# Second feed-forward stage: down product from fp16 parts, issued two tiles behind, low halves on VectorE

## What is computed

```python
def ffn(x):                                    # x: (4, 1024, 128) after a layer norm
    weights = routing_weights(x, Wr, temperature)      # (b, t, 8), from sigmoid and top 2
    gate = einsum('btd,edi->beti', x, Wg)              # 8 experts, 128 inner features each
    up   = einsum('btd,edi->beti', x, Wu)
    h = silu(gate) * up
    e_out = einsum('beti,eid->betd', h, Wd)            # the down product
    return einsum('bte,betd->btd', weights, e_out)

x = x + 0.5 * ffn(layernorm(x))
x = x + attention(layernorm(x))                # 16 heads of 64, latent q and kv, rope
x = x + 0.5 * ffn(layernorm(x))                # the second feed-forward stage
```

## Time and profile before

| | |
|---|---|
| median of 3 runs | 1598.68 us (1597.41 to 1603.1) |
| the profiled execution | 1597.2 us |
| its span | 1595.4 us, mean granted clock of TensorE 0.988 |
| TensorE matmul busy | 1536.4 us, 96% |
| VectorE busy | 1392.0 us, 87% |
| GpSimd busy | 1300.1 us, 81% |
| ScalarE busy | 1219.4 us, 76% |
| second feed-forward stage, turns 0 to 3 | about 1443 to 1595 us of the span |

### The profile page before, as it was taken

One profiled execution on the slowest core, in us unless ns is written; L12 is line 12 of the kernel. 1 busy time (PEld: TensorE's weight loads), 2 busy tenths in 40 slices (PEclk: granted clock), 3 DMA queues, 4 the chain that ended last, 5 costly groups with the idle time before them and its releaser, 6 DMA issues.

```text
span 1595.4 us, 47669 instructions
## 1 busy us (share of the span) xinstructions
PE 1536.4 (96%) x18968; PEld 1018.3 (64%) x18968; DVE 1392.0 (87%) x2860; ACT 1219.4 (76%) x1698; POOL 1300.1 (81%) x910
## 2 busy tenths in 40 slices
PE   5999779999999999999999999999999999989999
PEld 3777435666666666666666666666666666656776
DVE  7567788999999999999999999999999998966453
ACT  4443477888888888888888888888888888883432
POOL 2555356999999999999999999999999997764555
PEclk9999989999999999999999999999999999999999
DMA  7333030212121111212121212111121212003343
GB/s 209 114 115 119 27 80 11 52 32 55 46 54 42 41 42 42 55 39 51 32 51 32 60 42 53 42 41 42 45 55 35 51 32 52 22 2 107 121 136 117
DMA packets 65723, 95.63 MB, mean 60 GB/s; under 512 B 11744, under 2 KB 24544, under 8 KB 65248
## 3 DMA queue, kind: packets, MB, share of 16 engines
q1 hardware_dynamic: 62416, 91.66, 21.4%
q10 hardware_dynamic: 3088, 0.92, 0.3%
HBM read 39.72 MB, written 2.36 MB: 26 GB/s over the span
## 4 chain that ended last, share of the span: by engine, by line
PE 79%; DVE 3%; ACT 2%; POOL 2%; issue 2%; DMA 0%; POOLq 0%; SPq 0%; DVEq 0%
PE ps L965 14%; PE ps L939 14%; PE ps L966 14%; PE ps L985 8%; PE ps L987 8%; PE ps L983 8%; PE ps L954 3%; PE ps L490 2%; PE ps L947 2%; PE ps L933 2%; PE ps L932 2%; POOL area L617 1%; DVE area L1098 1%; PE ps L474 1%; PE ps L476 1%
## 5 line engine op out<-in xcount | busy, mean ns | idle before, releaser
L1303 POOL TENSOR_TENSOR area<-area 128x1024 f16<-128x1024 f32 (+1 forms) x512 | 833.0, 1645 | 89.2 <-ACT area L1223 79.5
L1098 DVE TENSOR_REDUCE area<-ps 128x1 f32<-128x512 f32 x1024 | 665.1, 685 | 10.0 <-PE ps L939 7.6
L1221 ACT ACTIVATE area<-ps 128x1024 f16<-128x1024 f32 x512 | 525.1, 1026 | 141.8 <-PE ps L966 141.5
L985 PE MATMUL ps<-cv_all,area 128*128 128x64 f16 x4096 | 457.6, 195 | 0.0
L983 PE MATMUL ps<-cv_all,area 128*128 128x65 f16 x4096 | 455.7, 193 | 0.6 <-POOL area L1303 0.5
L987 PE MATMUL ps<-cv_all,area 128*128 128x65 f16 x4096 | 454.6, 193 | 0.0
L985 PEld LDWEIGHTS ps<-cv_all,area 128*128 128x128 f16 x4096 | 381.9, 97 | 79.0 <-issue 0.3
L983 PEld LDWEIGHTS ps<-cv_all,area 128*128 128x128 f16 x4096 | 384.6, 97 | 59.5 <-issue 9.0
L939 PE MATMUL ps<-area 128*128 128x512 f16 x1024 | 389.0, 381 | 5.6 <-DVE area L1098 5.3
L965 PE MATMUL ps<-area 128*128 128x512 f16 x1024 | 389.4, 380 | 2.3 <-ACT area L1223 0.6
L966 PE MATMUL ps<-area 128*128 128x512 f16 x1024 | 389.7, 381 | 0.0
(11 more groups left out here) (182 smaller groups left out, 2169.5 us busy)
## 6 DMA issues: line engine op xcount, KB each, us to landing
area<-area SPq DMA_DIRECT2D x384, 128.0 KB, 2.7
area<-f_w_rows_in_dram SPq DMA_DIRECT2D x126, 256.0 KB, 3.2
xg<-in_x SPq DMA_DIRECT2D x4, 512.0 KB, 9.6
out_x<-xg SPq DMA_DIRECT2D x3, 512.0 KB, 4.7
area<-in_wup SPq DMA_DIRECT2D x1, 1024.0 KB, 8.8
cs<-in_rope SPq DMA_DIRECT2D x1, 1024.0 KB, 9.5
area<-area SPq DMA_DIRECT2D x64, 2.0 KB
area<-in_wg SPq DMA_DIRECT2D x1, 512.0 KB, 6.8
```

The costliest lines, as they stand in the source:

```text
L985: nc.tensor.matmul(o[:, 0:DH], p_hi[:, s % 4, c:c + P], latents[:, DH + 1:CV], start=False, stop=False, skip_group_check=True)
L1098: nc.vector.tensor_reduce(mx[:, hd, kh, qt:qt + 1], bank, AX.X, ALU.max).then_inc(s_mr, 1)
L1221: nc.scalar.activation(p_hi[:, s % 4, :], sc, ACT.Exp, scale=0.125).then_inc(s_e16, 1)
L1303: nc.gpsimd.tensor_tensor(p_lo[:, s % 4, c0:], src[:, (s // 2) % 2, :], p_hi[:, s % 4, c0:], ALU.subtract).then_inc(s_pp, 1)
```

## The change

- The first stage is left as it is, but for four operations: in its turns 1 and 2, `down_high` (ScalarE, step 13) and `down_low` (GpSimd, step 15) make fp16 high and low parts of the down weights, each for 4 experts.
- In the second stage hw is also split: ScalarE copies it to fp16 (`hw_hi`), VectorE subtracts (`hw_lo`), three buffers each. The down product is high times high, high times low, low times high, 12 fp16 products of 128 columns in place of 4 of fp32.
- Down runs two tiles behind (`lag = 2`): TensorE's step k is gate_up of tile i+2, then down of tile i-2. VectorE makes the low half of tile i-1 right behind hw of tile i. The last turn ends with two more downs.
- In the second stage the preparation of the next turn is moved: the transposes go to bank 5, at step 1 and at step 15 of the turn before (in the first turn steps 0 and 1); `normed` runs a turn ahead, at steps 8 and 9, in the first two turns, and at steps 0 and 1 of the first turn ahead of silu; hi at steps 0 and 2, router at 3, logits and tanh at 4, route with 6 links a step from step 5 (was 8 from step 7), weight_rows and rows at 10, add_y at 2 and 10.

```diff
+        wd_hi, wd_lo = sb("wd_hi", [P, E, P], F16), sb("wd_lo", [P, E, P], F16)
...
-        big = 30 * 1024
+        big = 30 * 1024 - 800
...
+        def down_high(act, n):
+            act.wait_ge(s_w[3], 16)
+            nc.scalar.copy(wd_hi[:, 4 * n:4 * n + 4, :], wd32[:, 4 * n:4 * n + 4, :]).then_inc(s_wdh, 1)
+
+        def down_low(pool, n):
+            pool.wait_ge(s_wdh, n + 1)
+            part = slice(4 * n, 4 * n + 4)
+            nc.gpsimd.tensor_tensor(wd_lo[:, part, :], wd32[:, part, :], wd_hi[:, part, :], ALU.subtract).then_inc(s_wdl, 1)
...
+            if name == "f2":
+                hw_hi, hw_lo = (carve(3 * 512, F16).rearrange("p (s n) -> p s n", s=3) for _ in range(2))
...
+            lag = 0 if first else 2
...
-                return 6 if first and p == 0 and a == 1 else 7
+                return 6 if first and p == 0 and a == 1 else 5 if not first and p > 0 else 7
...
+                    elif first and p > 0:
+                        pe.wait_ge(s_y, 2 * p - 1)
                     elif p > 0:
-                        pe.wait_ge(s_y, 2 * p - 1)
+                        pe.wait_ge(s_wt, p)
...
+                    if not first and p > 0:
+                        pe.wait_ge(s_y, 2 * p - 1)
...
-                    pe.wait_ge(s_hw, i + 1)
+                    if first:
+                        pe.wait_ge(s_hw, i + 1)
+                    else:
+                        pe.wait_ge(s_wdl, 2)
+                        pe.wait_ge(s_hl, i + 1)
                     for j in range(4):
...
+                            nc.tensor.matmul(o, hw_hi[:, i % 3, tokens], wd_hi[:, e, :], start=(e == 0 and j == 0), stop=False,
+                                             skip_group_check=True)
+                            nc.tensor.matmul(o, hw_hi[:, i % 3, tokens], wd_lo[:, e, :], start=False, stop=False, skip_group_check=True)
+                            last = nc.tensor.matmul(o, hw_lo[:, i % 3, tokens], wd_hi[:, e, :], start=False, stop=(e == E - 1),
+                                                    skip_group_check=True)
...
-                        if not last and k == 5:
+                        if not last and k == (5 if first else 3):
                             router(t + 1)
-                        down(i, t, k, last)
-                        if not last and k in (1, 3):
-                            transpose(t + 1, (k - 1) // 2)
-                        if not last and k == 11:
+                        if first:
+                            down(i, t, k, last)
+                        elif k >= lag:
+                            down(i - lag, t, k - lag, last)
+                        elif t > 0:
+                            down(i - lag, t - 1, 16 + k - lag, False)
+                        if first and not last and k in (1, 3):
+                            transpose(t + 1, k // 2)
+                        if not first and not last and (k == 1 or k == 0 and t == 0):
+                            transpose(t + 1, k)
+                        if not first and t < B - 2 and k == 15:
+                            transpose(t + 2, 0)
+                        if not last and k == (11 if first else 10):
                             weight_rows(t + 1)
+                    if last and not first:
+                        down(t * 16 + 14, t, 14, True)
+                        down(t * 16 + 15, t, 15, True)
...
+                        if not first and t == 0 and k < 2:
+                            normed(1, k)
                         if not (last and k == 15):
                             silu(i + 1, *((t, k + 1) if k < 15 else (t + 1, 0)))
+                        if not first:
+                            act.wait_ge(s_hw, i + 1)
+                            if i > 0:
+                                act.wait_ge(s_dn, i)
+                            nc.scalar.copy(hw_hi[:, i % 3, :], hw[:, k % 2, :]).then_inc(s_hh, 1)
...
+                        if first and t in (1, 2) and k == 13:
+                            down_high(act, t - 1)
                         if not last:
-                            if k in (0, 1):
+                            if first and k in (0, 1):
                                 normed(t + 1, k)
-                            if k in (2, 4):
-                                hi(t + 1, (k - 2) // 2)
-                            if k == 6:
+                            if not first and t < B - 2 and k in (8, 8 + 1):
+                                normed(t + 2, k - 8)
+                            if k in ((2, 4) if first else (0, 2)):
+                                hi(t + 1, (k - 1) // 2 if first else k // 2)
+                            if k == (6 if first else 4):
...
-                            if k == 11:
+                            if k == (11 if first else 10):
                                 rows(t + 1)
...
+                        if first and t in (1, 2) and k == 15:
+                            down_low(pool, t - 1)
...
+                def low_half(i):
+                    v.wait_ge(s_hh, i + 1)
+                    if i > 0:
+                        v.wait_ge(s_dn, i)
+                    nc.vector.tensor_tensor(hw_lo[:, i % 3, :], hw[:, i % 2, :], hw_hi[:, i % 3, :], ALU.subtract).then_inc(s_hl, 1)
...
-                    after_[1].append((lambda: add_y(t, 1)) if t > 0 else (lambda: v.sem_inc(s_y, 1)))
-                    after_[9].append(lambda: add_y(t, 0))
+                    after_[1 if first else 2].append((lambda: add_y(t, 1)) if t > 0 else (lambda: v.sem_inc(s_y, 1)))
+                    after_[9 if first else 10].append(lambda: add_y(t, 0))
...
+                        between[3 if first else 1].append(lambda: lo(t + 1, 0))
+                        between[5 if first else 3].append(lambda: lo(t + 1, 1))
+                        after_[6 if first else 4].append(lambda: logits(t + 1))
+                        jobs = [(route(t + 1), {k: 8 for k in range(7, 11)} if first else {k: 6 for k in range(5, 12)})]
...
-                        v.wait_ge(s_dn, i + 1)
+                        if first:
+                            v.wait_ge(s_dn, i + 1)
+                        elif i >= 2:
+                            v.wait_ge(s_hl, i - 1)
                         nc.vector.tensor_tensor(hw[:, b, :], gw[:, b, :], ps[:, 2 + b, :], ALU.mult).then_inc(s_hw, 1)
+                        if not first and i > 0:
+                            low_half(i - 1)
...
                     turns(turn)
+                    if not first:
+                        low_half(16 * B - 1)
                     add_y(B, 1)
```

More of the change, by code:

```diff
@@ L412, in turn @@
                         weights_to_all(t * 16 + k, t, k)
-                        if not last and k == 15:
+                        if not last and k == (15 if first else 15):
                             rows_out(t + 1)
@@ L451, in weight_rows @@
                     pe.wait_ge(s_routed, p + 1)
-                    if p > 0:
+                    if first and p > 0:
                         pe.wait_ge(s_y, 2 * p)
-                    nc.tensor.transpose(ps[0:E * TB, 6, 0:P], w_by_expert.rearrange("p e t -> p (e t)"), ident[:]).then_inc(s_wr, 1)
+                    nc.tensor.transpose(ps[0:E * TB, 6 if first or p == 0 else 5, 0:P], w_by_expert.rearrange("p e t -> p (e t)"), ident[:]).then_inc(s_wr, 1)
                 def row_on_all(k):
@@ L487, in down @@
                             pe.wait_ge(s_zr, t + 2)
-                    pe.wait_ge(s_hw, i + 1)
-                    for j in range(4):
-                        last = nc.tensor.matmul(ps[:, 6 + k // E, P * j:P * j + P], hw[:, b, P * j:P * j + P], wd32[:, e, :],
-                                                start=(e == 0 and j == 0), stop=(e == E - 1), skip_group_check=True)
+                    if first:
[3 more added lines that the diff above has]
+                        pe.wait_ge(s_hl, i + 1)
+                    for j in range(4):
+                        o, tokens = ps[:, 6 + k // E, P * j:P * j + P], slice(P * j, P * j + P)
+                        if first:
+                            last = nc.tensor.matmul(o, hw[:, b, tokens], wd32[:, e, :], start=(e == 0 and j == 0), stop=(e == E - 1),
+                                                    skip_group_check=True)
+                        else:
+                            nc.tensor.matmul(o, hw_hi[:, i % 3, tokens], wd_hi[:, e, :], start=(e == 0 and j == 0), stop=False,
+                                             skip_group_check=True)
+                            nc.tensor.matmul(o, hw_hi[:, i % 3, tokens], wd_lo[:, e, :], start=False, stop=False, skip_group_check=True)
+                            last = nc.tensor.matmul(o, hw_lo[:, i % 3, tokens], wd_hi[:, e, :], start=False, stop=(e == E - 1),
+                                                    skip_group_check=True)
                     last.then_inc(s_dn, 1)
@@ L562, in rows @@
                     act.wait_ge(s_wr, p + 1)
```

(14 more changed lines are left out.)

3 lines of the change are left out of this document (added).

## The result

The changed kernel takes 1600.96 us (median of 20 runs, 1599.77 to 1605.65), the kernel before 1598.9 us (20 runs beside it): ratio 1.0016, 95% interval 1.0009 to 1.0024. It is slower by 2.6 us, a sixth of a percent, and lies inside the bound of 0.5% that I called no change. The forecast was 1600.9 us. That the two agree to a tenth of a microsecond is luck: executions of the changed kernel differ by up to 6 us.

A forecast was written before the change was run, and what follows sets the result against it. TensorE alone was taken to bound the second feed-forward stage. The terms -14.0 (down), +13.4 (stalls), +2.5 (start) and +0.3 (tail) sum to +2.2 us, giving 1600.9 us, range 1587 to 1613.

The forecast's parts named there:

- The down product: Second stage, TensorE: 12 fp16 products take 0.67 us instead of 0.89 for fp32, 64 times, -14.0 us.
- Quiet tiles: Second-stage tiles without preparation: GpSimd product plus low half need 1.96 us, just within TensorE's 1.97, so they cost nothing.
- The sum of the stalls: First three turns of the second stage: TensorE stalls of 5.8, 3.8 and 3.8 us, together +13.4 us.
- hi and lo: First three turns: second hi cast behind step 2's copy, lo in front of hw(3), which delays hw(3) by 0.45 us.
- tanh: First three turns: logits behind a low half, then tanh and abs in front of silu(6), 1.0 us.
- Routing: VectorE, steps 7 to 9 of the first three turns: links with hw and low half cost 1.7 us a turn.
- Normed: ScalarE, first two turns: normed ahead of silu(10) and silu(11); the first hides behind routing, the second shows with 0.6 us.
- Start: Second stage's start: silu(2) queued behind copy, hi and normed(1, 1), so hw(2) ends late, +2.5 us, bounds 0 and 4.
- Tail: Behind the last hw: +1.65 us, less two lagging downs (1.33 us) filling TensorE's waiting, +0.3 us.
- A: Faster rival: the stalls overlap, only the worst of each turn counts, 5.1 us, no start; 1590 us, chance 0.25.
- B: Slower rival: the shared SBUF read bounds each quiet tile at 2.16 us, in all +10.6; 1609 us, chance 0.27.
- C: Rival: each pair costs its 98 ns load, down takes 1.18 us, no gain, +19 us; 1617 us, chance 0.03.

The follow-up runs named there:

- e1: Changed kernel with the low half's first input taken from a constant block in PSUM instead of hw in SBUF: 1594.5 us, ratio 0.9964.
- e6: Changed kernel without the high times low product of the down weights, 8 small products a tile instead of 12: 1601.46 us, ratio 1.0012.
- e7: Changed kernel with both edits, two of three down products and the low half's first input from PSUM: 1584.49 us, ratio 0.9906.
- e4: Changed kernel without the eight normed activations at steps 8 and 9 of turns 0 and 1: 1600.33 us, ratio 1.0001.
- e10: Changed kernel with one instruction moved, silu of tile 2 ahead of ScalarE's copy of tile 0: 1600.31 us, ratio 1.0012.
- e2: Changed kernel without the routing's small linked VectorE operations in the second stage's turns 0 to 2: 1595.53 us, ratio 0.9973.
- e9: Kernel before, with fp16 down, copy, low half and lag only for the first 14 tiles of the last turn: 1596.1 us, ratio 0.9983.
- e8: Changed kernel reordered: VectorE's links ahead of the low half; on ScalarE silu(i+2) ahead of the copy, hi and tanh ahead of that silu: 1604.71 us, ratio 1.0033.

## Why the prediction was right, and where its steps were not

**The signs.** They came as listed: down products spaced 55 ns, quiet steps of 1.97 us, a last turn of 29.66 us for 15 steps (31.6 for 16; I had 31.5), the first three at 36.3 to 39.5 us, low halves from 0.68 to 1.77 us, and no change in the first stage and the attention.

**The down product: right.** 12 small products in 0.67 us, a step of 1.97 us, -3.12 us in the last turn's 15 steps where 15 x 0.218 = 3.27 was due. L954 was the right row to take the price from. The sentence from the Trainium skill that pointed the other way ("TensorE: Matmul & The Clock Gate", section "Back-to-back issue gap", about 81 ns a pair) does not hold here: the pairs follow each other every 55 ns.

**Quiet tiles: right in cost, the second bound by another way.** I put TensorE at 1.97 and the excluding pair at 1.27 + 0.69 = 1.96 us and let the quiet tiles cost nothing. They cost nothing, and the square of e1, e6 and e7 shows a second bound at that height. But the pair itself takes 1.82 us when the low half waits (1574.78 to 1576.60). What stands at 1.94 us is the loop of two tiles in e6's timeline. The prediction names its part on ScalarE (silu(i+2) behind the copy of tile i, which waits for hw(i)) and never adds the loop up; that its height is that of the pair is chance.

**The sum of the stalls: right in size.** Turn by turn they are what the turns gave less the 16 x 0.218 = 3.5 us of the product: 7.6, 4.6 and 2.9 us, together 15.0; predicted were 15.9 with the start (8.3, 3.8 and 3.8). The end of the stage, from the first hw to the end of the span, came out at +2.6 us against +2.2.

**What the stalls are made of: wrong in one term.** I worked the steps of the routing with hw and low half at 0.60 us each. The exclusion, which I had in the quiet tiles, is at nothing there, and the prediction gives no reason for it. The turn's timeline of the changed kernel, steps 9 and 10, shows what happens:

```profile
1511.10 1.27 POOL L671 TENSOR_TENSOR area<-area 128x512 f32<-128x512 f32 x1 [2.45 <-ACT area L612]
1511.17 1.75 DVE L761 TENSOR_TENSOR area<-area 128x512 f16<-128x512 f32 x1
...
1513.69 0.68 DVE L817 TENSOR_TENSOR area<-area,ps 128x512 f32<-128x512 f32 x1
1514.01 1.26 POOL L671 TENSOR_TENSOR area<-area 128x512 f32<-128x512 f32 x1 [1.64 <-ACT area L612]
1514.29 1.54 DVE L761 TENSOR_TENSOR area<-area 128x512 f16<-128x512 f32 x1
...
1514.43 0.39 PE L493 MATMUL ps<-xt_hi,wu_hi 128*128 128x512 f16 x1 [0.98 <-DVE area L817]
```

GpSimd is not idle. ScalarE is late itself here (normed), so the product starts late, just as hw ends, and the low half behind hw pays for nearly all of it: 1.75 us, with the links and the next hw queued behind. By e1 the exclusion costs 7.8 us of the 15. My terms for hi and lo, tanh, routing and normed hold part of it each. Without the exclusion hw(9) to hw(10) of turn 1 takes 2.09 us (e1), with it 3.12; I had 2.3. Without normed, and with the exclusion, it takes 2.05 (e4): the excess needs both, the late product and the low half that waits for it. e1's expectation, 0 to 3 us, repeated the same mistake.

**Single terms.** Routing: 1.7 us a turn and 0.7 in the first, 5.8 in all; left out it gives 6.0 by the turns. Normed: 0.6 twice, measured 0.7 and 1.5. Start: 2.5, of which the order that I named explains 0.7 (e10). Tail: +0.3 predicted, +1.19 in the profile by my cut at the last hw. I had let the two downs of the lag fill TensorE's waiting there. The changed kernel's timeline shows it waiting for low halves ahead of them and between them:

```profile
1592.57 0.22 PE L518 MATMUL ps<-wd_hi,area 128*128 128x128 f16 x1 [0.90 <-DVE area L761]
...
1593.99 0.22 PE L518 MATMUL ps<-wd_hi,area 128*128 128x128 f16 x1 [0.59 <-DVE area L761]
```

These errors have both signs, and that the total is off by only 0.4 us is in part luck. Two slips of arithmetic are small: the links of the routing are given as 6.2 us in all and add up to 6.7 by steps (the forecast uses the steps), and the range by its own terms would run from about 1589 to 1611 us, not 1587 to 1613.

**The rivals.** A (delays overlap, 5.1 us in all) falls with e2 and with the 15.0 us of stalls. B had the right resource and the wrong place: it is not each quiet tile at 2.16 us that costs, but the low half caught in a step where VectorE has more to do. C falls with the last turn. What remains open is how the 7.8 us of the exclusion split between the terms of the preparation. By the distances from hw to hw with and without the shared read, the 3.2 us of turn 1 lie in steps 4 to 6 (0.6), 8 (0.3), 9 (1.0), 11 (0.6) and 12 to 15 (0.8); no run told apart what holds them there.

## What to carry to other kernels

Before moving work to an engine that is idle on average, look at the steps in which it isn't, and at what is queued behind the moved operation there: this change kept nearly its whole gain, 3.1 us, in the turn without preparation, kept 0.6 us in one of the others and lost 5.1 us in the first two, and the version that applied it only in the last turn (e9) was faster than both kernels. When an edit that should help shows nothing, suspect two bounds of one height, and take both away at once in a run of its own. Add up the loops that cross engines as well as each engine's own work. A VectorE operation with two inputs in SBUF is not independent of GpSimd; its price is a range (here 0.68 to 1.77 us), and which end it takes depends on what the rest of the schedule makes late.

## What the runs showed of the hardware that I had not expected

The exclusion works both ways. In the changed kernel 46 of 64 low halves take over 0.8 us, up to 1.77, beside products of 1.27; 44 of them, all whose product has a record of its own, end 0.53 to 0.56 us behind that product. In the other order a product took 1.72 us behind a low half of 0.68 and ended 1.14 us after it (e8). Either way one is held until the other is nearly through: the pair takes 1.82 us from start to end (1574.78 to 1576.60, and 1508.66 to 1510.48 in e8), 0.13 less than 1.27 + 0.68. It vanishes with one of VectorE's inputs in PSUM: 64 of 64 at 0.682 to 0.692 us (e1). That a low half with both inputs in SBUF takes 0.68 us when it is not disturbed, the same as with one in PSUM, was an assumption of the prediction and is now a row. The Trainium skill ("SBUF — State Buffer", "Who interferes with whom") says that a VectorE instruction with two inputs in SBUF contends with a GpSimd instruction that reads SBUF, and one with at most one such input does not; by that, all of these rows agree.
